# Four places for a slot's exponentials, and an order of steps with value products in pairs

## What is computed

```python
# l0: 32 score heads over 16 value heads
scores = einsum('bhtd,bhsd->bhts', q * scaling, k)
attn_w = softmax(scores, axis=-1)
attn_w = attn_w[:, :, 0] - lambda_full * attn_w[:, :, 1]
attn = einsum('bhts,bhse->bhte', attn_w, v)
# l2 (and f2 in the same way): 16 heads
scores = einsum('bhqd,bhkd->bhqk', q, k) / sqrt(HD)
attn = softmax(scores, axis=-1)
out = einsum('bhqk,bhkd->bhqd', attn, v)
# the whole
x = x + tanh(g_xattn[i]) * xattn_i(layernorm(x), ctx)
x = x + tanh(g_ffn[i]) * ffn_i(layernorm(x))      # i = 0..3
```

## Time and profile before

| | us |
|---|---|
| median of 3 runs | 4502.43 |
| lowest, highest | 4487.78, 4503.43 |
| span of the profiled execution | 4493.2 |
| busy: TensorE | 4197.2 (93%) |
| busy: DVE | 2949.1 (66%) |
| busy: ACT | 2085.8 (46%) |
| busy: POOL | 91.9 (2%) |
| mean granted clock of TensorE, share of full | 0.972 |

### The profile page before, as it was taken

One profiled execution on the slowest core, in us unless ns is written; L12 is line 12 of the kernel. 1 busy time (PEld: TensorE's weight loads), 2 busy tenths in 40 slices (PEclk: granted clock), 3 DMA queues, 4 the chain that ended last, 5 costly groups with the idle time before them and its releaser, 6 DMA issues.

```text
span 4493.2 us, 73928 instructions
## 1 busy us (share of the span) xinstructions
PE 4197.2 (93%) x28256; PEld 3198.6 (71%) x28256; DVE 2949.1 (66%) x7812; ACT 2085.8 (46%) x3424; POOL 91.9 (2%) x180
## 2 busy tenths in 40 slices
PE   7898998989989899898999999999999999999998
PEld 4675966759667596675966759667696676956768
DVE  6667776676656666666765767657676576665655
ACT  4544455353553435535355353553535535356342
POOL 0000000000000000000000000000000000000000
PEclk8999999999999999999999999999999999999999
DMA  2010610103001030010300103001030010300012
GB/s 99 1 45 10 217 37 1 52 23 132 29 15 41 24 128 29 15 41 29 123 29 15 41 29 123 29 15 41 29 123 29 15 41 29 123 29 15 31 55 102
DMA packets 51769, 228.06 MB, mean 51 GB/s; under 512 B 4832, under 2 KB 21216, under 8 KB 31584
## 3 DMA queue, kind: packets, MB, share of 16 engines
q1 hardware_dynamic: 51424, 223.33, 13.8%
HBM read 202.34 MB, written 20.97 MB: 50 GB/s over the span
## 4 chain that ended last, share of the span: by engine, by line
PE 80%; DVE 12%; ACT 5%; issue 3%; DMA 0%; SPq 0%; DVEq 0%; ACTq 0%
PE w L574 18%; PE w L584 12%; PE o L709 11%; PE w L830 8%; PE w L820 8%; PE w L642 4%; PE w L558 4%; PE o L702 3%; DVE mx L1243 3%; PE w L625 3%; PE w L677 2%; PE w L567 2%; PE w L721 1%; DVE nt L1184 1%; PE w L612 1%
## 5 line engine op out<-in xcount | busy, mean ns | idle before, releaser
L1243 DVE TENSOR_REDUCE mx<-w 128x4 f32<-128x1024 f32 x512 | 606.8, 1221 | 180.5 <-PE w L625 167.2
L975 ACT ACTIVATE pt_spread<-w 128x1024 f32<-128x1024 f32 x512 | 519.9, 1024 | 236.8 <-PE w L642 203.7
L709 PE MATMUL o<-pt_spread,va 128*32 128x256 f32 x4096 | 543.2, 396 | 30.5 <-ACT pt_spread L975 29.8
L921 ACT ACTIVATE oth<-w,res 128x256 f32<-128x256 f32 x656 | 276.9, 471 | 569.4 <-PE w L820 470.3
L574 PE MATMUL w<-xnT,stream 128*128 128x256 f32 x1792 | 413.1, 382 | 1.4 <-ACT xnT L913 0.8
L574 PEld LDWEIGHTS w<-xnT,stream 128*128 128x128 f32 x1792 | 338.2, 191 | 50.7 <-DVE x L1212 1.0
L709 PEld LDWEIGHTS o<-pt_spread,va 128*32 128x32 f32 x4096 | 205.0, 111 | 202.2 <-issue 63.3
L820 PE MATMUL w<-qodd,va_hi 128*128 128x256 f32 x2048 | 344.8, 283 | 1.1 <-issue 0.8
L820 PEld LDWEIGHTS w<-qodd,va_hi 128*128 128x128 f32 x2048 | 284.6, 188 | 7.8 <-issue 2.4
L1502 DVE TENSOR_REDUCE mx<-w 128x2 f32<-128x1024 f32 x128 | 155.8, 1225 | 199.2 <-PE w L679 198.9
L1212 DVE SCALAR_TENSOR_TENSOR x<-w,gate,x 128x256 f32<-128x256 f32 x512 | 223.2, 477 | 90.6 <-PE w L830 71.7
(11 more groups left out here) (263 smaller groups left out, 7722.5 us busy)
## 6 DMA issues: line engine op xcount, KB each, us to landing
stream_lo<-split SPq DMA_DIRECT2D x56, 1024.0 KB, 4.8
va_hi<-split SPq DMA_DIRECT2D x56, 1024.0 KB, 6.9
stream<-in_moe_dram SPq DMA_DIRECT2D x80, 384.0 KB, 3.1
stream<-in_resident_dram SPq DMA_DIRECT2D x8, 2048.0 KB, 7.4
raw<-in_moe_dram SPq DMA_DIRECT2D x8, 1024.0 KB, 6.8
split<-va_hi SPq DMA_DIRECT2D x8, 1024.0 KB, 8.9
split<-stream_lo SPq DMA_DIRECT2D x8, 1024.0 KB, 10.8
stream<-in_resident_dram SPq DMA_DIRECT2D x8, 1024.0 KB, 4.7
```

Of the source, the lines that this page charges most:

```text
L709: mm = pe.matmul(o[g:g + 32, 0:T], by_heads(plan, s)[:, kt, plan.v_of(h), :], p[:, a * 512 + kt * T:a * 512 + (kt + 1) * T], start=(kt == ...
L921: h = act.activation(dst[:, c, :], w[:, c * T:(c + 1) * T], func, bias=bias[:, c:c + 1], **more)
L975: act.activation(exp_buffer(plan.name + ".exp", s, u), w[:, :], ACT.Exp, scale=scale).then_inc(S["s_P"], 1)
L1243: dve.tensor_reduce(mx[s][:, :, 2 * v:2 * v + 2].rearrange("p t a -> p a t"), w[:, :].rearrange("p (a t k) -> p a t k", a=2, t=TT), AX_X, ...
```

## The change

The constant `SPREAD_EXPS` = 4 is the depth of the rings of l0, l2 and f2; l1's ring keeps its two places. The third place of a slot lies over `turned2` (`lent_turned`), the fourth over `qodd` (`lent_odd`); each has 1024 columns of f32 on 128 partitions, as one place of `pt_spread`. An exponential now waits for the value product four back in its ring. The string `ORDER` is another one throughout: the same 5032 steps in another order. The function `shared` returns two lists of buffers over the same memory.

```diff
-EXPS = 2
+EXPS, SPREAD_EXPS = 2, 4
...
-    "DAM11ADM11ADDAAMAAAA7AAAJAMAAAAAAAMA1AMMAMAD0M050M50M505M0M50M50M50M5M0550M50M50M5M0M505M0M55CC5HC0HCHCHCHCHC2H0CH0CHHC0"
...
+    "DAM11ADM11ADDAAMAAAA7AAAJAMAAAAAAAMA1AMMDAAM0M0M0M550M050M055M0M50M550M500MM550M0M550055MMM55CC5CCHHCCH0CHH2CCHHH0CH0CCH"
...
-        qodd = per_slot("qodd", [P, 4, T], F32R)
+        qodd, lent_odd = shared("qodd", [P, 4, T], F32R, "lent_odd", [P, 1024])
...
-        turned2 = per_slot("turned2", [P, TT, 512])
+        turned2, lent_turned = shared("turned2", [P, TT, 512], F32, "lent_turned", [P, 1024])
...
-            return pt[:, n % EXPS, :] if ring == 0 else pt_spread[s][:, n % EXPS, :]
+            if ring == 0:
+                return pt[:, n % EXPS, :]
+            if n % SPREAD_EXPS < EXPS:
+                return pt_spread[s][:, n % SPREAD_EXPS, :]
+            return (lent_turned if n % SPREAD_EXPS == EXPS else lent_odd)[s][:, :]
...
-                if n >= EXPS:
-                    last, ls, lu = EXP_STEPS[ring][n - EXPS]
+                depth = EXPS if ring == 0 else SPREAD_EXPS
+                if n >= depth:
+                    last, ls, lu = EXP_STEPS[ring][n - depth]
```

More of the change, by code:

```diff
@@ L273 @@
[L273 to L274 removed]
+    "DAM11ADM11ADDAAMAAAA7AAAJAMAAAAAAAMA1AMMDAAM0M0M0M550M050M055M0M50M550M500MM550M0M550055MMM55CC5CCHHCCH0CHH2CCHHH0CH0CCH"
+    "H7CCHHCCH0H062HH0H6060C6002C0C00C0CJ0ICIC00IEC0CI0C000CCEC02CC00CEC0C0C0CB0CBC00EB0B05C00B5005C505BC05B00CC5C0BN05C0NCC5"
@@ new lines @@
+    "NCCHNCNCHCCHN7C5CHCH0NN0CHC0HCHC3H0H0C30C00939008C980C9686698JCCCCLL6C86KCKLILCKI0LICKKI098L900KI8906C869I988CL3666C0LKL"
+    "C0KILIKKII000C0F0FC00CF00F0000C0C00C0A50C05C0C550C0CC055CC5C55C0C0CC0CHC7HHC0H000000C00C0C000HHHH0HJ0C000C0A0C0055CC0CCC"
+    "CC5CC50CC0C0CC55CC0CC555C0CC0C0HCCHBCHHCCHH00HHHBGC07CCC4C009CCC8L60K9BCI80L9KC6LB48IKJIG069CL86BK0IC9L186BKI0D91CLB8116"
+    "KAI09AMCA8BD6A09MDLA8K60C0LAAKDIJ0ICM00AAD0ACA7A0M0CM1AAC0AC0AAAA0AAAM0C0MC0050050C550MM550M0MCM0M550M5MCMM550M0M055MMMC"
@@ new lines @@
+    "MM5500CC55CC57CHHCC0HHCHCH2CCHH0CH02CHC0HHCCHHH0C60HH0EH0C606602C0C0CE00C0CIIC00IC0CIC000J0C200CEC0CCC0C0C0CBC0E0BCB0C0C"
+    "B0500B500550CB50C50B0CC5C0B0N5C0NCNC5CCHNCNCH7CH5CHCH0NCN0CCHHNC0C3HC3H0H0C303CF0909008C908C968869CCCLJ6CC6LK8K6CLKCII0L"
+    "KLI90IK90898806I09C6968L6860CCKLC00LKIIKIL0CLKK0IIC000FC0CF00F0000C0C00C0A05C05C0C550C0C0C55CC5C55C0C0C0CCCHA7CHH0C00000"
+    "0HH00C00H0C0HH0H0C000C0CJ000055C0CCCCCC0CC50CC5C05CC5CC55C7C54C00CC04C0C0HHCCHMHCCHH01HH0JH1CGC1C1CCG0C9ACCL8KIAC60L9KAI"
@@ new lines @@
+    "86DAAC0LK98AIC6L09KI86AAC0LK9IAA86A09CL86KIAAA0A9CAA8LAM06K978I6C0D0LAD0KJAI00DCM0D0CM0CMAC0MACC0C0C1MM000M0M0M550M550MC"
+    "0M0550M55MMCM500M0550M55M0MCMM5500C55CC75CCH0HCCHHCCH2CHHHC0HC0CHHCC0HHCCHH0H6H0H6062060C02C0CC000C00IC0CI0ICIE0CC0E0J20"
+    "0C0ECC0CCC0C0C0CBC0ECB00B00C5CB00B500550CB50C50B0CCC50BN05C0NCC5NCNCHCCHNC5CHHC0HN7N0CCCHHNC0C3HC3H3H0C300C00F99008C8996"
+    "0C68986CCCCL6CLK8ILKKCICLK60LI09KI09890I686980CC6L89LK68CKCJI60LC0LIKKLIIK0I000CFF000F0000C00CC0000ACC055C0C0CC055C0C550"
@@ new lines @@
+    "CCC555C0C0C7CH0CHCHM0CH0C00000HH00CC000HH0H00CJM000C0000C5CA0CCCCCC05CC0CC50C550CC5CC55C7C45C04CC0HCC00C0HHCCHHC1H0HH0H1"
+    "CGC1C1CCJA0C9GACC8ALK6DAI09ACLA86KAI09CL86KID09C8L6KID0C9L86AAKIAAC0L9K8I6AA09ACL8KAI6097DAA860CML0AAA0KIJ001C000MCDMCMM"
+    "0CCM00AAM0C0MC00505C0050M55M0M50M550M5C0M0M55M0055MMCMMCMM5500CC55CC5CHHCCHHCCHCHH0HC0H0CCHHCCHH0CCH2H0H6H0HC206066002C0"
+    "C0JC00CI70C0EII0C0CI0CC0E0CC002CCC0C0EC0C0C0CB0CB00E0CCB05B0BC05005505BC05B00CC5C0BN0C50NCNC5CCNHCCHNCCHNCC5HC0HN7N0CHCC"
@@ new lines @@
+    "0C00CII0ICI0C0EE02C0C00ECC0CCC0C0C0CBC0CB00CBC5C00E05B05CB00CCC50NBC055C0B0HNC50BNC05CH0NCNC5CNC7HC5CHCH0NCN00HCHC3CHH0H"
+    "3C003C0903F9008C98906C88966CCCL6CCLKLCKCLIK0J9ICKI0L8IL86690KC0LI9889066K9I86860KCLCCK0IL0LKKIII00CF000F00F00CC000C0C0CC"
+    "00C0C0C550C0550C055CCC5575C0C0CCCHCCHH00C000000H00C00HHC000HHH00C0J0C00C00055C0CCCCCC55CC0C0CC50CC5CC55C4C5C0CCCCHCHHCCH"
+    "C0H0HHH0H07CC0CCC00C9CC8LK60I9CL8K609IC8LK6CJ0LIK98G6ICL09KI8CL06K984I60C9L8K06C9IL860KIC00GC00C0C0CC0C00CC0CC0C"
```

61 lines of the change are left out of this document (20 added, 41 removed).

## The result

The changed kernel takes 4462.67 us (median of 4 runs, 4455.96 to 4466.27), the kernel before in the same comparison 4497.83 (4 runs, 4487.78 to 4503.43). The ratio is 0.992, with a 95% interval of 0.9902 to 0.9938: faster by 0.8%, 35 us, where 110 were forecast. The profiled spans, 4493.2 and 4454.2, differ by 39.0.

What follows compares the result with a forecast made beforehand. The prediction took TensorE, busy 93% of the span, as the bound. Its stage terms summed to 13.7 us a pass, 110 in eight, so 4502.4 - 110 = 4392 us, with a range of 4335 to 4470.

Steps and rivals of the forecast that it cites:

- The price of a pair: Value products: the second unit of each new pair is nearly free, 0.97 us saved, 183 us at 189 pairs as ceiling.
- Line 713 at 321 us: Value products (line 709 before): the union of their rows was to fall from 543 to 321 us.
- l0, slot a: First attention, slot a: seven new pairs, pace some 2.5 us a pair set by DVE and ACT; 5.0 us won a pass.
- l0, slot b: First attention, slot b: six new pairs, ACT's 2.43 us a pair as pace, f0 using little; 2.0 us won a pass.
- l2, slot a: Slot a's values in l2: four new pairs, a pair from 3.56 to 2.59 us; 3.2 us won a pass.
- f2 and l2's slot b: Three terms won a pass: l2 slot b until f2's exponentials 1.0 us, f2 slot a 0.8, f2 slot b 1.7.
- Part 2: Exponentials in l0, l2 and f2 get four ring places: put at 0, within a few us either way.
- Part 3: Moved steps in f0, l1, f1 and f2's experts: put at 0, within 3 us a pass (24 in all) either way.
- evacuation binds: Rival, chance 0.27: DVE and ACT set the pace wherever pairs stand and filler doesn't help; 66 us won, 4436.
- Slower, waits in front of each pair: Rival, chance 0.07: TensorE stands still for the second unit's exponential at each pair; 4540 us at full price.
- Into the chains: Rival, chance 0.08: time saved becomes waits in f0, l2 and f2, or moved steps cost as much; 4480 to 4525.
- The warning sign on f0: The prediction was to count as wrong if f0's stage grew by more than 3 us.

Runs made afterwards that it cites:

- light_after: The changed kernel with the attentions' exponentials and maxima halved from the second pass on (other heads left out): 4372.77 us.
- light_before: The kernel before with the attentions' exponentials and maxima halved from the second pass on (other heads left out): 4443.01 us.
- ring4_old_order: The changed kernel with the order string of the kernel before, so only the four ring places are new: 4498.6 us, ratio 1.0002 to the kernel before.
- old_order_pairs: Four ring places and the old order, with each even unit's value product moved directly ahead of the next unit's: 4466.33 us.
- splice_l0: Four ring places, old order, but l0's exponentials to values in the new order, and pairs by rule in l2 slot a and f2 slot b: 4430.46 us.
- new_order_singles: The changed kernel with the first value product of some 185 pairs moved ahead of the exponential step before it: 4619.44 us.
- same_columns: The changed kernel with both units of a pair on the same column groups, so they can't overlap (half the heads' values left out): 4568.87 us.
- after_filler: The changed kernel with 128 more f32 matmuls, ahead of slot a's scores for the maxima of l2 and f2: 4481.87 us.
- some pairs against all: Four ring places, old order, value products paired except in l2 slot b and f2 slot a, 4445.64 us, against old_order_pairs, 4466.33.

## Why the prediction came out as it did

**The direction and the range held; the size didn't.** 35 us were won, 7 us inside the near end of 4335 to 4470. The terms of the sum came to 12.2 us a pass for 13.7, which is luck: slot b of l0 brought 5.4 too much, slot a of l0 and the f2 terms 2.4 and 4.1 too little. What made 110 into 35 stood outside the sum.

**The price of a pair was right.** The work of value products fell by 177.4 us at 189 new pairs, 0.94 each against 0.97; the gap is in the broken pairs (20 of 170). That all work fell by 182.8, just the 183 computed, has some luck in it: 8.5 of it are score products, which had been put at no change.

**Line 713 at 321 us: 366 measured,** because some 30 of its pairs ran at the low clock (36 us of the difference) and some were broken. Busy time down by 130 to 180: 98.9, for the same reason. The term was in the unit of the full clock, and nobody had asked what the clock would be.

**l0, slot a: 2.6 us a pass for 5.0.** The pace of 2.5 was reached in places only. DVE's timeline there, where the earlier trace rows had 0.26:

```profile
1174.45 1.23 DVE L1248 TENSOR_REDUCE mx<-w 128x4 f32<-128x1024 f32 x1 [1.39 <-PE w L629]
1176.28 1.23 DVE L1248 TENSOR_REDUCE mx<-w 128x4 f32<-128x1024 f32 x1 [0.60 <-PE w L629]
1178.19 1.23 DVE L1248 TENSOR_REDUCE mx<-w 128x4 f32<-128x1024 f32 x1 [0.69 <-PE w L629]
```

DVE was expected to lose its idle time, and it grew: maxima wait for scores. In PE's timeline scores wait in turn:

```profile
1186.36 0.50 PE L629 MATMUL w<-ksp,qsp 32*128 32x256 f32 x4 [0.76 <-DVE tmp L1291]
```

The sum took DVE's and ACT's totals as the pace; in this order neither was kept fed. Whether the six banks or the sequence of steps is behind it isn't shown. With the work of both halved (light_after against light_before) the stage won 4.4 us a pass.

**l0, slot b: 7.4 us a pass for 2.0**, the largest term missed in the other direction. (The stage ends at the last exponential, and some value products and other work now stand behind it: f0's work grew by 12.4 us over the passes. f0 gave back 0.7 us a pass, where the prediction had let it take most of slot b's gain.) ACT's timeline:

```profile
1205.55 1.02 ACT L980 ACTIVATE pt_spread<-w 128x1024 f32<-128x1024 f32 x1
1206.45 0.39 ACT L917 ACTIVATE oth<-o 128x256 f32<-128x256 f32 x1
1206.71 1.05 ACT L980 ACTIVATE lent_turned<-w 128x1024 f32<-128x1024 f32 x1
1207.62 1.06 ACT L980 ACTIVATE lent_odd<-w 128x1024 f32<-128x1024 f32 x1
1208.52 1.07 ACT L980 ACTIVATE pt_spread<-w 128x1024 f32<-128x1024 f32 x1
```

Back to back, ACT's rows start 0.91 us apart and last 1.02 or more; the same place in two pairs, 1204.62 (just ahead of these rows) and 1206.71, is 2.09 us apart, not the 2.43 that three durations add up to. The Trainium skill says so ("ScalarE: Activation LUTs", What ACT_TABLE_LOAD costs: back-to-back ACTIVATEs overlap by about 93 ns); the trace agrees roughly, with 0.12 to 0.16 us in these rows, and the sum should have gone by starts and not by durations. Part of this may also rest on ACT no longer waiting for banks and products, 0.40 in the earlier trace rows.

**l2, slot a: 2.8 for 3.2;** right. (In l2 a unit's two heads take both halves of the array's rows, so the parity of units makes no difference there, other than the text ahead of the prediction has it.) **f2 and l2's slot b: -0.6 for 3.5 together** (l2 b until f2's first exponentials -0.9 for 1.0, then 0.1 for 0.8 and 0.3 for 1.7). The work of f2's three stages fell by 69 us over the passes (58 new pairs stand there, 56 us by the price above); time at half clock (+99, half of which is added time) and idle time (+27) took it back.

**Part 2 at 0: right,** shown by ring4_old_order.

**Part 3 at 0, within 3 us a pass: the step that failed.** What lies outside the terms above cost 7.3 us a pass: the experts 4.3, l2 ahead of its exponentials 1.7, l1 1.4, f0 0.7; f1 alone gave 0.6. The prediction bounded this part by the idle time that f0 and l2 had to take or give. But the experts had TensorE at 99%, and could only get worse: their idle time went from 5.9 to 22.8 us and their half-clock time from 0 to 27.9. With the old order there they take 812.2 us again, whether or not pairs stand elsewhere (old_order_pairs, splice_l0); with the new order they take 846.7 though pairs are undone (new_order_singles) and 840.3 though pairs don't overlap (same_columns). That the order causes it is shown; which moved step does is not.

**The clock had no term at all,** the second thing that the sum lacked. The prediction read 0.91 in f0 and 0.86 in l2 and took them as given. Half-clock time grew by 167 us, most in f2 until slot a's exponentials (+58) and the experts (+28), and the ledger puts 84 us on it, of which some part isn't lost time (after_filler). It comes with packing (same_columns has 76 us less of it than the changed kernel) and with the place (some pairs against all: -124).

**The rivals.** The result lies in the band of *evacuation binds* (22 to 80 us won, 4436 as its figure), but that mechanism is only a part of it (70 us won with the evacuation halved, 35 with all of it). *Slower, waits in front of each pair* is refuted for this kernel (3.4 us of idle time before the products); a form of it does happen in the old order, hidden inside the pairs. *Into the chains* had two halves: waits in f2, which came (+27 us idle, with the clock beside them), and moved steps that cost, which is what Part 3 missed; it had a chance of 0.08, at the price of the whole gain. No rival had the clock. The warning sign on f0 (3 us a pass) stayed silent, at +0.7.

**Open:** which moved step costs in the experts, l1 and l2 (the new order in the experts alone wasn't tried); how the 84 us of clock divide into lost time and time in which TensorE would have waited anyway; how f0 could use what slot b wins.

## What to carry to other kernels

When TensorE's work shrinks, keep three accounts, work at full clock, half-clock time and idle time: here the first fell as computed and the other two ate four fifths of it. Pack where other work lies beside the chain, leave the spots where TensorE waits for small steps as they are, and don't re-lay stages that have nothing to win: less packing was faster twice. For an engine's pace take the distance between starts of back-to-back rows, not the sum of their durations.

## What the runs showed of the hardware

Matmuls on disjoint column groups of one bank overlapped even when both of a group's are issued in a row: sixteen f32 rows took 1.02 us to the next start, against 1.87 on shared groups. Rows of the two units started in turns, four column groups at a time, and not in the order in which they had been given.

The clock fell in places where TensorE had only short gaps. Ahead of one half-clock stretch of f2, the changed kernel's PE timeline has score steps with gaps of about 0.4 us, and then rows that are longer, the last of these by a factor of nearly two:

```profile
1503.86 0.50 PE L629 MATMUL w<-ksp,qsp 32*128 32x256 f32 x4
1504.73 0.50 PE L629 MATMUL w<-ksp,qsp 32*128 32x256 f32 x4 [0.37 <-ACT lent_turned L980]
1505.65 0.79 PE L629 MATMUL w<-ksp,qsp 32*128 32x256 f32 x4 [0.42 <-ACT lent_odd L980]
...
1508.98 1.97 PE L725 MATMUL w<-res,oth 128*128 128x128 f32 x8
```

In the kernel before the same eight rows (of line 721) take 1.06 us. Windows ahead of the stretch and of the stretch itself:

```profile
1501.40:1505.40 4.00, 2.91 (x30) 1.77 (x24) 1.31 (x2) 3.11 (x5) 0.00 (x0) 1.00 0.01 4
1505.40:1519.10 13.70, 12.85 (x66) 9.20 (x67) 10.13 (x14) 1.77 (x4) 0.89 (x2) 0.50 0.00 0
```

Inside the stretch TensorE is busy 94% of the time and still runs at half clock; the busy share of a stretch alone doesn't tell its clock. The Trainium skill ("TensorE: Matmul & The Clock Gate", A second HAM failure mode: psum-queue depth-cycling) describes a kernel in which frequent very short waits between groups of matmuls made the clock swing between its two levels. This trace agrees in kind, with 77 half-clock stretches where there were 41, and by that rule the forecast would have needed a term of its own for them.
